# A four-block post-norm kernel: state products in 32-column strips, the last pair in two units, and a shorter warm-up

## The reference

```python
x = layernorm(x + attn0(x))   # 16 heads of 8; q, k: rmsnorm and rope; pattern = (q.k / 8)^2 * causal; z = pattern @ v; x + z @ Wo.T
x = layernorm(x + ffn0(x))    # every operand quantised to FP4 in blocks of 16; silu(x @ Wg.T) * (x @ Wu.T) @ Wd.T, inner width 352
x = layernorm(x + attn1(x))   # g = gelu(x @ keys.T), 512 keys; g / |g| * sqrt(512) @ values
x = layernorm(x + ffn1(x))    # gelu(x @ w1 + b1) @ w2 + b2, inner width 512
```

## Time and profile before

| | |
|---|---|
| median of 3 runs | 228.06 us (227.95 to 228.82) |
| the profiled execution | 228.60 us, its span 226.8 us |
| TensorE busy (matmul / weight load) | 204.1 / 154.5 us |
| VectorE busy | 190.0 us |
| ScalarE busy | 133.8 us |
| POOL busy | 86.4 us |
| granted TensorE clock, mean | 0.989 |

### The profile page before, as it was taken

How to read it: one execution, slowest core, us unless ns; L and a number is a source line. 1 busy time by engine, 2 the same in 40 slices (tenths; PEclk the granted TensorE clock), 3 DMA queues, 4 the chain that set the end, 5 groups by cost and what they waited for, 6 DMA issues and landing times.

```text
span 226.8 us, 5511 instructions
## 1 busy us (share of the span) xinstructions
PE 204.1 (90%) x1905; PEld 154.5 (68%) x1905; DVE 190.0 (84%) x516; ACT 133.8 (59%) x257; POOL 86.4 (38%) x124
## 2 busy tenths in 40 slices
PE   8945978898899799899999999999999999999980
PEld 8713455475657476777677869667897978888780
DVE  0299999999998999999889978997899998554444
ACT  0089579759784778377693774864353475343620
POOL 5003442309208319321633573065544033445251
PEclk9999699999999999999999999999999999999998
DMA  6920010010001000000000000000010000010001
GB/s 203 356 88 0 4 31 20 0 49 0 3 1 46 3 26 0 0 6 0 4 0 3 0 3 1 3 0 4 13 36 1 0 3 0 0 49 0 25 27 46
DMA packets 6075, 5.99 MB, mean 26 GB/s; under 512 B 1440, under 2 KB 5408, under 8 KB 6048
## 3 DMA queue, kind: packets, MB, share of 16 engines
q1 hardware_dynamic: 5184, 4.99, 6.9%
q10 hardware_dynamic: 864, 0.65, 0.9%
HBM read 4.58 MB, written 1.05 MB: 25 GB/s over the span
## 4 chain that ended last, share of the span: by engine, by line
PE 52%; issue 20%; DVE 16%; POOL 6%; ACT 3%; POOLq 0%; DVEq 0%; ACTq 0%
PE psum L326 9%; PE psum L415 7%; PE psum L557 4%; PE psum L339 3%; PE psum L456 3%; PE psum L603 3%; PE psum L366 3%; PE psum L332 3%; POOL ln_rstd L2014 3%; PE psum L511 2%; PE psum L521 2%; ACT pat L819 2%; POOL ln_veps L2009 2%; DVE x L1320 2%; PE psum L434 1%
## 5 line engine op out<-in xcount | busy, mean ns | idle before, releaser
L2046 POOL TENSOR_SCALAR_AFFINE_SELECT pat<-pat 128x1024 f32<-128x1024 f32 x32 | 40.1, 1272 | 56.7 <-ACT pat L819 56.7
L819 ACT ACTIVATE pat<-psum 128x1024 f32<-128x1024 f32 x32 | 31.6, 1029 | 13.8 <-PE psum L415 13.5
L2009 POOL TENSOR_TENSOR ln_veps<-ln_mv,ln_eps 128x2 f32<-128x2 f32 x32 | 9.4, 296 | 59.4 <-DVE ln_mv L1314 59.4
L2014 POOL TENSOR_TENSOR ln_rstd<-ln_veps,minus_half 128x2 f32<-128x2 f32 x32 | 23.4, 736 | 1.6
L415 PE MATMUL psum<-q_wide,k_t 32*128 32x512 f32 x128 | 18.4, 642 | 4.9 <-DVE v_raw L1341 1.8
L1320 DVE TENSOR_SCALAR x<-y,ln_mv,ln_rstd 128x128 f32<-128x128 f32 x48 | 16.8, 393 | 5.2 <-POOL ln_rstd L2014 5.2
L819 ACT ACTIVATE h<-psum,b_sb 128x256 f32<-128x256 f32 x32 | 12.5, 476 | 10.3 <-PE psum L603 10.3
L326 PE MATMUL psum<-values,g 128*128 128x128 f32 x128 | 16.0, 278 | 0.7 <-DVE h L1489 0.7
L456 PEld LDWEIGHTS psum<-pat,v_wide 128*32 128x32 f32 x512 | 13.5, 110 | 4.5 <-issue 4.5
L326 PE MATMUL psum<-w_sb,h 128*128 128x128 f32 x128 | 15.8, 277 | 0.6 <-DVE x L1570 0.6
L326 PEld LDWEIGHTS psum<-values,g 128*128 128x128 f32 x128 | 15.1, 192 | 1.9 <-issue 1.8
(11 more groups left out here) (130 smaller groups left out, 484.9 us busy)
## 6 DMA issues: line engine op xcount, KB each, us to landing
xt_in<-in_x_t SPq DMA_DIRECT2D x8, 128.0 KB, 3.8
x_in<-in_x SPq DMA_DIRECT2D x8, 128.0 KB, 3.0
out_dram<-x SPq DMA_DIRECT2D x8, 128.0 KB, 1.7
w_sb<-in_w SPq DMA_DIRECT2D x2, 256.0 KB, 3.9
gu_raw<-in_w_gu ACTq DMA_DIRECT2D x1, 384.0 KB, 3.9
keys<-in_keys_t SPq DMA_DIRECT2D x1, 256.0 KB, 4.0
values<-in_vals SPq DMA_DIRECT2D x1, 256.0 KB, 4.8
wqkv<-in_w_qkv_t SPq DMA_DIRECT2D x1, 192.0 KB, 4.1
```

Source lines behind the costliest of these rows:

```text
L819: return nc.scalar.activation(dst, src, func, **kw)
L2009: pool.tensor_tensor(ln.veps[:, :], ln.mv[:, :, 1], ln_eps[:, :], ALU.add).then_inc(s[ln.name + "_veps"], 1)
L2014: pool.tensor_tensor(ln.rstd[:, :], ln.veps[:, :], minus_half[:, :], ALU.pow)\
L2046: pool.affine_select(out=part, in_=part, compare_op=ALU.is_ge, fill=0.0, base=0, pattern=[[0, 2 * HG], [1, P]], channel_multiplier=-1).the ...
```

## The change

Three edits, and new lists for all engines. `keep_warm` issues 9 products. The 64x128 products of `z_state` are each cut into four with 64x32 weights, which write to four strips of 32 PSUM partitions. From `output_projection` on, the last pair becomes two units: unit 7 is batch 0 of pair 7 and unit 8 is batch 1, each half as wide; the steps ahead of it still know eight pairs. The calls of units 7 and 8 are placed separately in the lists.

```diff
+LAST = PAIRS - 1
+UNITS = PAIRS + B - 1
...
+def batches(u):
+    return range(B) if u < LAST else range(u - LAST, u - LAST + 1)
+def before(u):
+    return u - 1 if u <= LAST else u - 2
+def own(u, width):
+    b = batches(u)
+    return slice(b[0] * width, (b[-1] + 1) * width)
...
-            for u in range(PAIRS):
+            for u in range(UNITS):
                 sp.wait_ge(s["ln4_out"], u + 1)
-                sp.dma_start(out[u, :, :], x4[u % 2][:, :]).then_inc(stored[u % 2], 16)
+                sp.dma_start(out[min(u, LAST), :, own(u, P)], x4[u % 2][:, own(u, P)]).then_inc(stored[u % 2], 16)
...
-            keep_warm(22)
+            keep_warm(9)
...
                 def from_last(b):
                     half = slice(b * NH * HALF, (b + 1) * NH * HALF)
-                    return pe.matmul(rows("z_state", u, b), st[half, STATE_A:STATE_W], last_t[u % 2][half, :], start=(b == 0),
-                                     stop=False, skip_group_check=True)
+                    for gr in range(NG):
+                        cols = slice(STATE_A + 32 * gr, STATE_A + 32 * gr + 32)
+                        mm = pe.matmul(rows("z_state", u, b)[32 * gr:32 * gr + 32, :], st[half, cols], last_t[u % 2][half, :],
+                                       start=(b == 0), stop=False, skip_group_check=True)
+                    return mm
...
             def output_projection(u):
-                pe.wait_ge(s["z_scaled"], u + 1)
+                pe.wait_ge(s["z_scaled"], min(u, LAST) + 1)
...
-                for b in range(B):
+                for b in batches(u):
...
                 for n in range(NC):
-                    mm = pe.matmul(at("ffn_up", u, 2)[:, n // 2, n % 2 * T:(n % 2 + 1) * T], w1_sb[:, n * P:(n + 1) * P],
-                                   x3_t[:, :], start=True, stop=True)
+                    mm = pe.matmul(at("ffn_up", u, 2)[:, n // 2, n % 2 * T:(n % 2 + 1) * T][:, own(u, P)],
+                                   w1_sb[:, n * P:(n + 1) * P], x3_t[:, own(u, P)], start=True, stop=True)
```

More of the change, by code:

```diff
@@ L831, in square_qk @@
                 act.wait_ge(s["bias_qk"], u + 1)
-                wait(act, "head_sums", u - 1)
+                wait(act, "head_sums", before(u))
                 if u == 0:
@@ L918, in copy_two @@
             def copy_two(stage, u, dst):
-                return act_op(dst[:, :], at(stage, u)[:, 0:T], ACT.Copy)
+                cols = slice(0, T) if stage == "transpose_rq" else own(u, P)
+                return act_op(dst[:, cols], at(stage, u)[:, cols], ACT.Copy)
             def copy_rq(u):
@@ L933, in tanh_gate @@
                 act.wait_ge(s["gate"], u + 1)
-                wait(act, "h_gate", u - 1)
-                act_op(th[:, :, :], at("gate", u, 2)[:, :, 0:I], ACT.Tanh, scale=0.5).then_inc(s["tanh_gate"], 1)
+                wait(act, "h_gate", before(u))
+                act_op(th[:, own(u, 1), :], at("gate", u, 2)[:, own(u, 1), 0:I], ACT.Tanh, scale=0.5).then_inc(s["tanh_gate"], 1)
             def copy_h(u):
@@ L1311, in norm_moments @@
                 dve.wait_ge(s[ln.name + "_sums"], u + 1)
-                wait(dve, ln.name + "_veps", u - 1)
-                for b in range(B):
+                wait(dve, ln.name + "_veps", before(u))
+                for b in batches(u):
                     op = dve.bn_aggr(ln.mv[:, b, :], ln.stats[:, b, :])
@@ L1361, in turn_cos @@
                 dve.wait_ge(s["bias_qk"], u + 1)
-                wait(dve, "turn_sum", u - 1)
+                wait(dve, "turn_sum", before(u))
                 if u == 0:
@@ L1590, in _ @@
             turn_sin(0)
+            head_sums(0)
+            turn_sum(0)
             bias_qk(1)
[L1592 to L1593 removed]
+            head_inverse(0)
             bias_v(1)
@@ L1614, in _ @@
+            multiply_last(1)
+            scale_v(0)
+            multiply_feats(0)
+            head_sums(1)
+            bias_qk(2)
+            bias_v(2)
+            qgu_inverse(0)
+            head_inverse(1)
+            turn_cos(2)
+            scale_v(1)
+            turn_sin(2)
+            qgu_divide(0)
+            turn_sum(2)
             head_sums(2)
-            qgu_inverse(0)
             bias_qk(3)
-            head_inverse(2)
+            bias_v(3)
+            take_state(0)
+            turn_sin(3)
@@ L1664, in _ @@
             qdown_out(0)
-            ln1_sums(1)
-            turn_cos(4)
-            ln1_moments(1)
-            turn_sum(4)
-            bias_v(5)
-            head_inverse(4)
-            bias_qk(5)
-            scale_v(4)
-            multiply_feats(3)
+            h_gate(0)
+            take_state(2)
+            h_up(0)
             bias_v(6)
             bias_qk(6)
-            take_state(2)
-            h_gate(0)
+            head_sums(5)
+            qh_amax(0)
+            multiply_feats(3)
@@ L1734, in _ @@
+            qx_out(2)
             ln1_sums(3)
-            qx_add(2)
+            scale_v(5)
+            turn_cos(6)
+            qh_subtract(1)
             ln1_moments(3)
-            qx_subtract(2)
-            head_inverse(5)
-            qx_out(2)
-            multiply_feats(4)
+            qh_out(1)
+            bias_v(7)
+            bias_qk(7)
+            head_sums(6)
+            h_gate(2)
+            take_state(4)
+            h_up(2)
+            turn_sum(6)
             ln2_in(1)
-            head_sums(6)
+            qh_amax(2)
@@ L1886, in _ @@
-            qh_subtract(5)
+            ln2_moments(4)
+            qh_inverse(5)
+            qx_inverse(6)
+            ln4_moments(0)
+            qx_divide(6)
+            qx_grid(6)
+            qx_add(6)
+            ln3_in(2)
+            qx_subtract(6)
+            qx_out(6)
+            qh_divide(5)
+            ln2_out(4)
+            qh_grid(5)
+            qh_add(5)
+            ln3_sums(2)
+            qh_subtract(5)
+            z_scaled(7)
+            qh_out(5)
+            h_gate(6)
@@ L1969, in _ @@
             ln4_moments(4)
-            ln3_out(6)
+            ln2_in(8)
+            ln2_sums(8)
+            ln2_moments(8)
+            ln2_out(8)
+            ln4_out(4)
+            ln4_in(5)
+            ln4_sums(5)
+            ln4_moments(5)
             ln3_in(7)
```

1367 lines of the change are left out of this document (707 added, 660 removed).

## The result

The changed kernel takes 222.14 us (median of 3 runs, 220.88 to 222.71) against 228.06: ratio 0.972, 95% interval 0.965 to 0.980. The forecast was 224.8 with a range of 221.5 to 228.8. The time is inside the range, yet nearest to rival (a), 222.4; why it is there has to be seen.

What follows compares the result with a forecast made beforehand. VectorE was taken to bound the kernel until 100 us, TensorE after it, then the run-out. Terms -2.4 (front), -0.5 (strips), -0.4 (waits at the end) gave -3.3 us, forecast 224.8, range 221.5 to 228.8.

Steps and rivals of the forecast that it cites:

- rival (a): More gain: cheaper strips, no wait at head_sums, shorter run-out, -4.7 us or 223.4; with the order's -1, 222.4; chance 0.18.
- Front: Kernel start: shorter warm-up lets VectorE become dense at 7.5 us, not 10.19; less 0.3 us at head_sums, net -2.4 us.
- Strips: z_state products: four strips take 0.35 us against 0.41, -0.06 each; eight sets where TensorE is the bound, -0.5 us.
- The rival price of 0.285 us: z_state: a group of four strips costs half a group of eight, -0.125 us each, -1.0 us in all.
- the serial one: z_state: strips do not run side by side; eight records take 1.64 us, +1.23 each and +9.8 us in that stage.
- Waits at the end: Last ffn_down's wait for gelu: halves remove 0.3 us of the gap, and as much at an earlier one; -0.4 together.
- Run-out: After the last product: shorter half steps save 0.6 us, POOL's second chain costs 0.9; taken as 0, bounds -0.6 and +0.4.
- Order: New engine lists and PSUM banks: little to win, as TensorE waits only 1.9 us after 100 us; zero, -1 to +3.
- (b): Clock eats the front: TensorE may be low for early transposes, projections and scores, 2.6 us; about 227.2, chance 0.14.
- Split: Last pair in two units: VectorE's +3.4 us is hidden below TensorE; zero taken, 0 to +1.5 in the range.
- (c): Slower: z_state strips run one after another, +9.8 us against the other -2.8, giving 235; chance 0.07.
- (d): New order leaves TensorE waiting in its dense stage, around quantiser chains of units 7 and 8: 3.6 us, 228.4; chance 0.09.

Runs made afterwards that it cites:

- e6: Kernel before with 9 warm-up products and the state's products in strips, own lists, no split: 225.12 us, ratio 0.9875 to before.
- e4: Changed kernel with every call of unit 8 struck out, so pair 7 is one unit again in the new lists: 228.41 us, ratio 0.9948 to before.
- e7: e4 with eleven products of the identity with itself ahead of transpose_x3(7), filling TensorE's long wait: 226.73 us, ratio 0.9900 to before.
- e5: Kernel before, its own lists, only the warm-up cut from 22 to 9 products: 227.15 us, ratio 0.9905 to before.
- E2: Changed kernel with 22 warm-up products again instead of 9: 223.88 us, ratio 0.9791 to before.
- E11: Changed kernel with the call of keep_warm removed, so no warm-up product at all: 222.08 us, ratio 0.9701 to before.
- e3: Changed kernel with the two 64x128 products of z_state whole again instead of strips: 222.87 us, ratio 0.9721 to before.
- E8: Changed kernel with unit 8 ending in its own buffer y1 and ln4_moments(7) ahead of ln4_in(8): 221.09 us, ratio 0.9672 to before.
- e12: Kernel before with all three edits in its own lists, unit 8's calls right behind unit 7's, separate banks for unit 8: 230.93 us, ratio 1.0095 to before.
- e1: The changed kernel again, unedited, as reference beside its variants: 222.29 us, ratio 0.9706 to before.

## Where the prediction was right, and why it was 2.7 us short

The balance at 100 us, each figure from rows above or worked out from them (run-out: span less end of the last product):

| kernel | work left at 100 us | TensorE waits behind it | last product ends | run-out |
|---|---|---|---|---|
| before | 119.6 | 1.8 | 221.5 | 5.3 |
| e6: warm-up and strips | 116.2 | 1.9 | 218.0 | 5.3 |
| after | 113.7 | 1.5 | 215.2 | 5.2 |
| e4: after, pair whole | 115.5, some 2.4 of it low clock | 5.1 | 220.6 | 6.2 |
| e7: e4 filled | 116.3, 2.6 of it filling | 2.7 | 219.0 | 6.0 |

*Front, forecast -2.4.* Right. The first bias came at 8.05 us (forecast near 8.4), the new wait at head_sums was 0.42 us (0.3); e5 gives -2.2 us. E2 takes 1.6 back, but that is weaker evidence, since only 0.65 of it lie in the span. The reason given was right too: VectorE's first work is what counts. E11 sharpens it: the gain is that thirteen products no longer stand ahead of project(0), and the nine that are left buy nothing.

*Strips, forecast -0.5.* Right, 0.35 us a set as worked out from the two group sizes; e3's +0.6 and e6 against e5 (-0.3% by the ratios) agree, both within their error. Behind 100 us lie six sets and not eight (48 records in e6 and in the kernel after), which is nearer -0.4. The rival price of 0.285 us and the serial one are out. "TensorEngine Tiling (Array Packing)" of the Trainium skill, section Key Properties, has a drain at each change of mode; the 0.13 us of entry did stay in the group of four, so the trace agrees.

*Waits at the end, forecast -0.4.* The balance has -0.35, and the gap before the last ffn_down went from 0.61 to 0.34 us, near the 0.3 that was said.

*Run-out, forecast 0.* The size was right (5.2 for 5.3), the reason only half of it. POOL's two chains do stand one behind the other: 0.54 and 0.55 us, where one root of double width took 0.69. But ln4_in(8) also waited for the store of unit 6, for which the prediction did not look: the step "ln4_in(8) waits for the last product" was wrong by 0.8 us. E8 removed both and the run-out fell to 4.1.

*Order, forecast 0 with -1 to +3, as a term apart from the split: the step that failed.* "There is little to win", it said, because TensorE waits only 1.9 us after 100 us. Order and split together gave 3.9 us by the ratios (0.9875 and 0.9706), with some 1.5 either way, where the sum had 0.4. An order can also win on the other side of 100 us, where VectorE is the bound and TensorE has 14.4 us empty: what TensorE gets done there is missing from the dense stage. The new lists leave 2.5 us less of its busy time than e6, most of the 2.9 us between the two spans. Not all of that is work done earlier. Busy time also holds the pauses at a change of tile size, and the new lists have 43 such changes behind 100 us, e6 46 (88 and 94 in all); at the 0.13 us of entry of the prediction that is 0.4 us. An estimate that prices the records left by their kind, at their rate in the dense stage of these traces (0.115 us for one of 128x128, 0.22 for 128x256), gives 107.5 us of products left in e6 and 106.3 in the kernel after, 1.2 us. The remaining 0.9 us is not accounted for, and single executions of one list differ by about as much (see (b)).

*Split, forecast as a term by itself.* That was the other half of the same error. Beside warm-up and strips, which all four have:

| | lists of before | new lists |
|---|---|---|
| pair 7 whole | e6: 0.9875 | e4: 0.9948 |
| pair 7 in two units | e12: 1.0095 | e1: 0.9706 |

Each alone is slower than neither, the new lists by 0.7%, just outside the error, and the split by 2.2%; only both are faster. The balance shows how for e4: with the pair whole the new lists bring no more work to 100 us (115.5 - 2.4 = 113.1 us at the full clock) and lose the lead at the end: 3.6 us in waits (5.1 against 1.5), 2.4 in the clock behind the longest of them, and 1.0 in the run-out. The lists put TensorE's other work ahead, so that nothing covers the last pair's chain of transposes, norms and gelus; half units cover each other. What stays open: e4's lists are those of the split with unit 8 struck out, e12's are the old ones with unit 8 added (and its entries in the bank table to match). Neither was arranged anew, so the runs show that these lists need the split, not that no order of a whole pair could do as well. One such order, ffn_down(6) and its gelu ahead of transpose_x3(7), was not run.

*The range.* That the time lies inside it owes something to luck. Its lower end took in most of rival (a), whose prices did not come; by the bounds for split and order alone the sum could fall to 223.8 only, and these two were what moved.

*Rivals.* (a) named the time, 222.4, by the wrong road: none of its three prices came (0.285 us a set, no wait at head_sums, -0.6 in the run-out); only its -1 for the order has the right sign, and is too small. (c) is out by the 0.35 us; (d) by 59.70 of 60.00 and 30.00 of 30.00 us in the stages of the quantisers. VectorE's dearer halves were covered, as forecast.

(b) has two parts. An early low stretch of the clock, of which it speaks, came in some executions and cost nothing. In e4 the granted clock was 0.74 and 0.50 from 12 to 16 us, in e7 1.00; e7 has e4's lists up to the filling, and VectorE's steps stand within 0.02 us of each other in the two until 29 us. A later one, at 24 to 28 us, came in the kernel before (0.50), in the kernel after (0.60 and 0.55) and in e7, but not in e4, and that one was not hidden. The stretch from 24 to 26 us and the VectorE step at which the two executions part, in e4:

```profile
24.00:26.00 2.00, 1.35 (x16) 0.58 (x20) 2.00 (x6) 1.82 (x6) 1.43 (x2) 1.00 0.02 4
...
30.37 0.42 DVE L1478 SCALAR_TENSOR_TENSOR y<-x_in,psum 128x256 f32<-128x256 f32 x1
```

and in e7:

```profile
24.00:26.00 2.00, 1.58 (x8) 0.55 (x8) 2.00 (x6) 1.44 (x4) 1.41 (x2) 0.54 0.01 4
...
31.05 0.42 DVE L1483 SCALAR_TENSOR_TENSOR y<-x_in,psum 128x256 f32<-128x256 f32 x1 [0.64 <-PE psum L521]
```

VectorE waits 0.64 us for TensorE. By 34 us it is 1.0 us behind e4, as one of its own steps also takes 1.48 us for 1.14, which no run explains, and it stays 1.0 us behind up to the filling. So even in the stage that VectorE bounds, TensorE's clock can cost about a microsecond, and two profiled executions of one list can lie that far apart. The profiled executions of the kernels before and after both had such a stretch.

## What to carry to other kernels

Where one engine bounds the first stage and another the second, ask of a new order how much of the second engine's work it gets done *before* the change-over; idle time in the second stage does not show that gain. A split of the last unit and the order of the lists are to be priced as one edit: each can cost time alone. Before a microsecond between two profiled executions is put down to an edit, compare the granted clock of the stretches ahead of it. Before counting on a shorter run-out, list what the last steps' *output buffer* waits for, not only their operands.

## What the runs showed of the hardware beyond that

The point at which TensorE rises to its higher level is not the same in each execution: the same 44 warm-up records took 7.75 us and 6.58 us in e2, as their weight loads went from 333 to 192 ns at 6.4 to 6.6 us in the one and at 3.8 to 4.2 us in the other. An estimate that hangs on it is as uncertain, here by about a microsecond.

POOL's power on one column per partition costs more than half of what two cost: 0.55 us, in the timeline of the end above, against 0.71 in the same kernel. Halving the unit does not halve this step (start us, us):

```profile
212.81 0.71 POOL L2117 TENSOR_TENSOR ln_rstd<-ln_veps,minus_half 128x2 f32<-128x2 f32 x1
```
